# Layer norms of layers 2 and 3 computed inside the loops of the stages before them, on one Trainium2 core

## The chip, the cores and the metric

The kernel runs on one core of one Trainium2 chip. The metric is the device time of one execution in microseconds (us). TensorE multiplies matrices out of SBUF into PSUM, VectorE and ScalarE work elementwise and read PSUM, GpSimd works elementwise on SBUF, SyncE issues the DMAs. In the profile they are PE (PEld for its weight loads), DVE, ACT, POOL and SP.

## The reference

Eight residual steps on x (8 batches x 256 tokens x 128 channels) with a context of 8 x 512 x 96:

```
for l in 0..3:
    x = x + Ll_xattn(_layernorm(x), ctx, ...)
    x = x + Ll_ffn(_layernorm(x), ...)
_layernorm: (x - mean) / sqrt(var + 1e-5), over the 128 channels
```

Each step needs `_layernorm` of the x that the step before has left, token by token. Those that matter here:

- L1_ffn: 8 experts; each has a fixed block of 128 tokens in each of 2 halves of the token list. `h = gelu(g @ w1 + b1)`, `y = h @ w2 + b2`, `out = gelu(y @ next_w + next_b)`.
- L2_xattn: 8 heads of 64, `softmax(q k^T / 8) v`, then `@ Wo + bo`. L3_xattn is the same with 16 heads.
- L2_ffn: q and k projections, their images under W_inv, a running sum of k over the tokens, a router (gelu, then softmax over 8), and per expert `(q V) * (cumsum(k) W) * weight`, summed through U and projected by W_O.
- L3_ffn: the two best experts of 8 per batch, chosen by its first token's normed x; the mean of their two feed-forwards is added.

## The kernel before

All tokens stay in SBUF as `g.x`, 16 tiles of 128 tokens (partitions) x 128 channels. Every stage is one or more blocks. A block has a program for each engine, the engines keep in step by semaphores, and all of them meet at a block's end; behind each stage `clear_semaphores` (L110) runs a block of its own. Within an engine all instructions run in the order of the text.

Four stages begin with the norm of all 16 tiles by the class `AllTiles` (L214): VectorE computes statistics (`bn_stats`, L252, `bn_aggr`, L257) of two halves of 8 tiles and adds epsilon (L261), GpSimd raises to the power -1/2 (L289), VectorE subtracts the mean and scales (L268), TensorE transposes 4 tiles into one PSUM bank (L296). What comes then differs:

- `split_heads` (L1226), ahead of `wide_attention` in layers 2 and 3: ScalarE copies each bank to `z_hi` in the reduced type fp32r (L1256), VectorE subtracts for `z_lo` (L1264), and GpSimd splits the weights wq, wk and wv in two in the same way (3 casts, L1246, then 3 subtractions, L1249). These raw weights are loaded at the start of the run with all others.
- `l2_ffn` (L1824), block l2f_front: ScalarE copies 512 transposed tokens at a time to a small `zT` (L1972). TensorE's steps are skewed by chunk: transposes, then the q and k products (L1922), then the W_inv and router products, then the logits (L1928). VectorE makes the running sums (L2014). GpSimd zeroes the stacked weights (L1894) and splits four tables (L1899, L1902). The softmax of all tokens starts with L2040.
- `l3_ffn` (L2209), block l3f_norm: ScalarE copies the transposed tokens to `zT` and the first token of each batch to `zT_first` (L2255, L2256). Then the router's scores (L2242).

The loops ahead of them:

- `l1_ffn` (L1612). Its block l1f_front norms twice and makes xaT; there SyncE loads w1 and w2 of the first two experts (L1632). The block l1f_experts has 4 turns of 2 experts. TensorE's turn is second(u, 0) (L1742), next_layer(u - 1) (L1750, L1751), second(u, 1), then hidden(u + 1) for both experts (L1733); next_layer of the last turn follows the loop. ScalarE: the gelu of next_layer's result (L1780), then 8 gelus of hidden (L1775). VectorE: keep_y(u, 0) (L1799, writes yT), update(u - 1) of x (L1806, 4 tiles), keep_y(u, 1). GpSimd has nothing.
- `wide_attention` (L1268). 8 turns, one per batch (2 tiles), each of C = HEADS/2 units c (pairs of heads). A unit's work, 4 blocks of 128 x 512 scores, is a chain: scores (TensorE, L1377), maxima (VectorE, L1532), exponentials (ScalarE, L1479), reciprocals (VectorE, L1538), scaling (GpSimd, L1333), and in the next unit the transposes (`turned`, TensorE, L1386) and their copies (u = 0, 2 by VectorE, L1544; u = 1, 3 by ScalarE, L1486), one later the weighted sum (L1397) and its copy (L1549). Between these stand the projections of the next unit: k (L1353), q (L1345) and v (L1362), whose results are split by ScalarE (L1467, L1462) and VectorE (`k_low` L1527, `q_low` L1522). The output projection of batch b - 1 (`joined`, L1406) ends unit 1 of batch b on TensorE, the update of x (L1555) ends it on VectorE.
- `l2_ffn`, block l2f_experts: 4 turns of 512 tokens (4 tiles), each of 8 steps n. TensorE: the products of step n + 1 (L2096, L2100, L2103), then out(u, n) (L2110), which needs VectorE's `prod` of step n; output(u - 1) (L2121) after n = 1. ScalarE copies xv (L2148). VectorE multiplies twice a step (L2178, L2182), splits q and cum at n = 1 and n = 5 (L2172, L2173), and updates x at n = 3 (L2187). xv and prod have two buffers each. GpSimd has nothing.

The print below is of the kernel before; the profile's line numbers are its own.

## Time and profile before

| | us |
|---|---|
| time, median of 3 runs | 1837.53 (1837.08 to 1838.91) |
| the profiled execution's own time | 1838.08 |
| its span, first to last instruction | 1836.2 |
| TensorE busy (matmuls) | 1523.5, 83% of the span |
| TensorE weight loads | 1073.8, 58% |
| VectorE busy | 1043.0, 57% |
| ScalarE busy | 952.4, 52% |
| GpSimd busy | 596.4, 32% |
| mean granted TensorE clock | 0.899 of full |

A row of the timeline gives the start in us from the span's start, the duration, engine, line, operation, what it writes and reads with shapes, the number of instructions merged in it (xN), and in brackets the idle time of the engine before it and what ended it. The duration of a merged row runs from the first start to the last end. Ends of matmuls are modelled. A matmul of fp32 counts as two instructions. Tile names start with the stage: l1f, l2w (split_heads of layer 2), l2a, l2f, l3w, l3a, l3f.

### The profile page before, as it was taken

The page shows a single profiled execution, that of the slowest core. Times are in us where ns is not written, and L with a number is a line of the kernel's source. Part 1 is how long each engine was busy: PE and PEld are TensorE (multiplying, and loading weights), DVE is VectorE, ACT ScalarE, POOL GpSimd, SP SyncE. Part 2 cuts the span into 40 slices and gives each one's busy share as a digit, 9 for nine tenths or more (in the row PEclk, how much of TensorE's full clock was granted, in tenths as well). Part 3 has the DMA queues.
Part 4 walks back from the last instruction along what each step waited for, and adds up shares of the span by engine and source line. Part 5 has one row for each costly group of instructions (what it writes and reads, how often), then busy time and mean ns, then how long its engine had stood idle before and what let it go on. Part 6 is the DMA issues. An engine that isn't in the chain of part 4 may idle for free. (4 is left out here: it accounts for less than half of the span.)

```text
span 1836.2 us, 31074 instructions
## 1 busy us (share of the span) xinstructions
PE 1523.5 (83%) x10011; PEld 1073.8 (58%) x10011; DVE 1043.0 (57%) x2401; ACT 952.4 (52%) x2022; POOL 596.4 (32%) x592
## 2 busy tenths in 40 slices
PE   3999984698348736689999978959999999999976
PEld 2555543597125524567677746736777777777754
DVE  3566635344657654455665655665566666666651
ACT  2787861342356463265665623315666566665642
POOL 3323313100000001255555530034554554555441
PEclk7999995799569957789999988978999999999997
DMA  5300000000000002100000000000000000000002
GB/s 150 80 0 0 1 1 1 1 1 5 18 1 1 0 1 64 29 1 0 0 0 0 1 1 1 1 0 1 1 1 0 0 0 0 0 0 0 1 2 69
DMA packets 28737, 19.84 MB, mean 11 GB/s; under 512 B 9128, under 2 KB 25716, under 8 KB 28660
## 3 DMA queue, kind: packets, MB, share of 16 engines
q1 hardware_dynamic: 28660, 18.87, 3.7%
q8 instruction: 42, 0.69, 0.2%
q14 instruction: 35, 0.29, 0.0%
HBM read 17.81 MB, written 1.05 MB: 10 GB/s over the span
## 5 line engine op out<-in xcount | busy, mean ns | idle before, releaser
L1333 POOL TENSOR_TENSOR l3a_prob<-l3a_prob,l3a_rinv 128x512 f32<-128x512 f32 x256 | 260.8, 1040 | 249.9 <-DVE l3a_rinv L1538 245.0
L1479 ACT ACTIVATE l3a_prob<-l3a_scores_ps,l3a_nmax 128x512 f32<-128x512 f32 x256 | 173.2, 683 | 137.9 <-DVE l3a_nmax L1532 137.9
L1532 DVE TENSOR_REDUCE l3a_nmax<-l3a_scores_ps 128x2 f32<-128x1024 f32 x128 | 150.8, 1219 | 87.6 <-PE l3a_scores_ps L1377 87.5
L1333 POOL TENSOR_TENSOR l2a_prob<-l2a_prob,l2a_rinv 128x512 f32<-128x512 f32 x128 | 130.3, 1040 | 123.7 <-DVE l2a_rinv L1538 122.7
L746 ACT ACTIVATE l0a_prob<-l0a_scores_ps,l0a_k_scale 128x1024 f32<-128x1024 f32 x128 | 142.4, 1114 | 38.0 <-PE l0a_pv_ps L640 35.3
L1386 PE MATMUL l3a_turned_ps<-const,l3a_prob 128*128 128x128 f32 x1024 | 156.3, 276 | 3.0 <-DVE l3a_probT L1544 0.9
L1386 PEld LDWEIGHTS l3a_turned_ps<-const,l3a_prob 128*128 128x128 f32 x1024 | 118.4, 141 | 26.8 <-DVE l3a_probT L1544 11.9
L1397 PE MATMUL l3a_work_ps<-l3a_probT,l3a_v 128*64 128x256 f32 x1024 | 124.6, 385 | 1.6 <-ACT l3a_probT L1486 0.9
L1479 ACT ACTIVATE l2a_prob<-l2a_scores_ps,l2a_nmax 128x512 f32<-128x512 f32 x128 | 86.6, 683 | 73.7 <-DVE l2a_nmax L1532 73.7
L1544 DVE COPY l3a_probT<-l3a_turned_ps 128x512 f32<-128x512 f32 x128 | 87.8, 686 | 56.5 <-PE l3a_turned_ps L1386 56.4
L1532 DVE TENSOR_REDUCE l2a_nmax<-l2a_scores_ps 128x2 f32<-128x1024 f32 x64 | 75.5, 1219 | 41.2 <-PE l2a_scores_ps L1377 41.1
L1397 PEld LDWEIGHTS l3a_work_ps<-l3a_probT,l3a_v 128*64 128x64 f32 x1024 | 68.3, 136 | 51.9 <-issue 23.6
L626 PE MATMUL l0a_scores_ps<-l0a_qS,l0a_kS 128*128 128x512 f32 x256 | 91.7, 440 | 0.2
L289 POOL TENSOR_TENSOR l1f_front_all_rstd<-l1f_front_all_var_eps,neg_half 128x8 f32<-128x8 f32 x4 | 6.8, 1700 | 236.8 <-DVE l1f_front_all_var_eps L261 236.8
L640 PE MATMUL l0a_pv_ps<-l0a_prob,l0a_v 128*32 128x256 f32 x1024 | 81.7, 391 | 0.8 <-ACT l0a_prob L746 0.8
L1386 PE MATMUL l2a_turned_ps<-const,l2a_prob 128*128 128x128 f32 x512 | 78.0, 276 | 2.3 <-DVE l2a_probT L1544 0.9
L1486 ACT ACTIVATE l3a_probT<-l3a_turned_ps 128x512 f32<-128x512 f32 x128 | 76.9, 601 | 4.8 <-PE l3a_turned_ps L1386 4.8
L1172 ACT ACTIVATE l0f_experts_hidden<-l0f_experts_hidden_ps,vectors 128x512 f32<-128x512 f32 x64 | 43.0, 687 | 59.7 <-PE l0f_experts_hidden_ps L1133 59.5
L1386 PEld LDWEIGHTS l2a_turned_ps<-const,l2a_prob 128*128 128x128 f32 x512 | 58.8, 140 | 14.8 <-DVE l2a_probT L1544 6.5
L1196 DVE SCALAR_TENSOR_TENSOR l0f_experts_acc<-l0f_experts_y_ps,l0f_experts_gate_chunk,l0f_experts_acc 128x128 f32<-128x128 f32 x112 | 31.5, 344 | 59.7 <-PE l0f_experts_y_ps L1149 59.7
L1397 PE MATMUL l2a_work_ps<-l2a_probT,l2a_v 128*64 128x256 f32 x512 | 62.3, 385 | 1.6 <-ACT l2a_probT L1486 0.9
L1471 ACT ACTIVATE l3a_v<-l3a_work_ps 128x512 f32<-128x512 f32 x64 | 38.2, 597 | 48.9 <-PE l3a_work_ps L1364 48.9
(607 smaller groups left out, 3807.4 us busy)
## 6 DMA issues: line engine op xcount, KB each, us to landing
l1f_w<-in_L_ffn_w SPq DMA_DIRECT2D x16, 256.0 KB, 2.9
l3f_experts_w<-in_L_ffn_W SPq DMA_DIRECT2D x32, 64.0 KB, 1.9
ctx_rows<-in_ctx SPq DMA_DIRECT2D x1, 1536.0 KB, 7.2
w_l_w<-in_L_ffn_W SPq DMA_DIRECT2D x1, 1024.0 KB
out_x<-x_tokens SPq DMA_DIRECT2D x1, 1024.0 KB, 4.5
w_l_wq<-in_L_xattn_Wq SPq DMA_DIRECT2D x1, 512.0 KB
w_l_wo<-in_L_xattn_Wo SPq DMA_DIRECT2D x1, 512.0 KB
l1a_raw_f<-in_L_xattn_W_f SPq DMA_DIRECT2D x1, 512.0 KB, 4.3
```

The costliest lines, as they stand in the source:

```text
L626: last = e.matmul(sc[n % 2][:, half * 512:half * 512 + 512], kS[:, grp, t * P:(t + 1) * P], qS[:, grp, 2 * half:2 * half + 2, :], start=Tr ...
L640: last = e.matmul(pvps[grp % 2][32 * j:32 * j + 32, 0:T], v[:, t, GH * grp + j, :], prob[n % 2][:, j * T:(j + 1) * T], start=t == 0, stop= ...
L746: e.activation(prob[n % 2][:, :], sc[n % 2][:, :], ACT.Exp, scale=kscale[:, n % KT:n % KT + 1]).then_inc(m.prob_ready, 1)
L1172: e.activation(h[x % 4][:, f, :], hps[n % (2 * FT)][:, :], ACT.Gelu, bias=g.l0_b1[:, n:n + 1]).then_inc(m.act_ready, 1)
L1333: e.tensor_tensor(prob[n][:, :], prob[n][:, :], bcast(rinv[:, n:n + 1], [P, S]), ALU.mult).then_inc(m.prob_ready, 1)
L1386: last = e.transpose(tps[u % 2][:, t * P:(t + 1) * P], prob[slot(c, u)][:, t * P:(t + 1) * P], g.ident)
L1397: last = e.matmul(work[0][HD * h:HD * h + HD, 0:T], v[:, t, head], pT[c % 2][:, t, h, :], start=t == 0, stop=t == KT - 1, tile_position=(0 ...
L1471: e.activation(v[:, c % 2 * 2:c % 2 * 2 + 2, c // 2 * 256:(c // 2 + 1) * 256], work[1][:, :].rearrange("p (t d) -> p t d", t=2), ACT.Copy) ...
L1479: e.activation(prob[at][:, :], bank(u), ACT.Exp, bias=nmax[:, at:at + 1], accum_out=rsum[:, at:at + 1]).then_inc(m.exp_ready, 1)
L1486: e.activation(pT[c % 2][:, :, u % 2, u // 2 * P:u // 2 * P + P], tps[u % 2][:, :].rearrange("p (t q) -> p t q", q=P), ACT.Copy).then_inc( ...
L1532: e.tensor_reduce(nmax[:, at:at + 2], sps[:, i * 1024:(i + 1) * 1024].rearrange("p (h k) -> p h k", h=2), AX.X, ALU.max, negate=True).then ...
L1544: e.tensor_copy(pT[c % 2][:, :, u % 2, u // 2 * P:u // 2 * P + P], tps[u % 2][:, :].rearrange("p (t q) -> p t q", q=P)).then_inc(m.pT_kept ...
```

## The change

The class `Ahead` norms one turn's tiles inside the loop of the stage before, into tiles that outlive the stage: `g.z_hi` and `g.z_lo` where an attention follows, `g.zT` (float32) where a feed-forward follows. `split_heads` and the four uses of `AllTiles` in layer 2, layer 3 attention and layer 3 feed-forward are deleted. The wq, wk and wv of layers 2 and 3 are no longer in the first load: `SplitWeights` loads them in block l1f_front (six DMAs, after the four expert loads) and splits them on GpSimd in block l1f_experts (six casts, six subtractions). In the loops' order:

- l1_ffn: TensorE's transposes of turn u - 1 stand at the end of turn u, ScalarE's copy too, VectorE's statistics, scaling and low part behind keep_y(u, 1); the last group behind the loop. GpSimd's power of group 0 stands behind the splits.
- wide_attention: VectorE's statistics of batch b - 1 stand behind the update at the end of unit 1, the scaling in unit 2 before the reciprocals, GpSimd's power at the head of unit 2, TensorE's two transposes at the end of unit 2 into `turned0`'s bank, ScalarE's copy at the end of unit 2; the first transposes of unit 3 wait for that copy.
- l2_ffn: statistics after n = 4, scaling after n = 5, transposes and ScalarE's copy after n = 6, low part after n = 7, in the bank of output's result. Its block l2f_front has no norm, no zT copies and no z banks; `w_stacked` is now two tiles, in z_hi and z_lo. xv and xy lie in `g.zT`.
- l3_ffn: block l3f_norm starts with the scores, read from `g.zT` with a stride.

The core of the diff:

```diff
+class Ahead:
+    def __init__(self, s, g, tiles):
+        self.g, self.tiles = g, tiles
+        self.stats = s.sb("ahead_stats", [P, tiles, 6])
+        self.mv = s.sb("ahead_mean_var", [P, tiles, 2])
+        self.var = s.sb("ahead_var_eps", [P, tiles])
+        self.rstd = s.sb("ahead_rstd", [P, tiles])
+        self.held = s.sb("ahead_held", [P, 1])
+        self.z = s.sb("ahead_z", [P, tiles, D])
+        self.x_counted = s.sem("ahead_x_counted")
+        self.var_ready = s.sem("ahead_var_ready")
+        self.rstd_ready = s.sem("ahead_rstd_ready")
+        self.z_ready = s.sem("ahead_z_ready")
+        self.z_turned = s.sem("ahead_z_turned")
+        self.z_kept = s.sem("ahead_z_kept")
+        self.z_lo_ready = s.sem("ahead_z_lo_ready")
+    def statistics(self, e, n, x, updated, count):
+        e.wait_ge(updated, count)
+        e.memset(self.held[:, :], 0.0)
+        for i in range(self.tiles):
+            e.bn_stats(self.stats[:, i, :], x[i]).then_inc(self.x_counted, 1)
+        e.wait_ge(self.x_counted, 2 * self.tiles * n + self.tiles)
+        e.memset(self.held[:, :], 0.0)
+        for i in range(self.tiles):
+            e.bn_aggr(self.mv[:, i, :], self.stats[:, i, :]).then_inc(self.x_counted, 1)
+        e.wait_ge(self.x_counted, 2 * self.tiles * n + 2 * self.tiles)
+        e.tensor_scalar(self.var[:, :], self.mv[:, :, 1], EPS, None, ALU.add).then_inc(self.var_ready, 1)
+    def gpsimd(self, e, n):
+        e.wait_ge(self.var_ready, n + 1)
+        e.tensor_tensor(self.rstd[:, :], self.var[:, :], self.g.neg_half[:, 0:self.tiles], ALU.pow).then_inc(self.rstd_ready, 1)
+    def apply(self, e, n, x):
+        e.wait_ge(self.rstd_ready, n + 1)
+        for i in range(self.tiles):
+            e.tensor_scalar(self.z[:, i, :], x[i], self.mv[:, i, 0:1], self.rstd[:, i:i + 1], ALU.subtract,
+                            ALU.mult).then_inc(self.z_ready, 1)
+    def tensor(self, e, n, out):
+        e.wait_ge(self.z_ready, self.tiles * (n + 1))
+        for i in range(self.tiles):
+            last = e.transpose(out[:, i * P:(i + 1) * P], self.z[:, i, :], self.g.ident)
+        last.then_inc(self.z_turned, 1)
+    def keep(self, e, n, out, src):
+        e.wait_ge(self.z_turned, n + 1)
+        e.activation(out, src, ACT.Copy).then_inc(self.z_kept, 1)
+    def low(self, e, n, out, src, high):
+        e.wait_ge(self.z_kept, n + 1)
+        e.tensor_tensor(out, src, high, ALU.subtract).then_inc(self.z_lo_ready, 1)
...
+    def sync(self, sp):
+        for n in self.NAMES:
+            sp.dma_start(self.raw[n][:, :], self.a[f"L{n[0]}_xattn_W{n[1]}"]).then_inc(self.loaded, 16)
+    def gpsimd(self, e):
+        e.wait_ge(self.loaded, 16 * len(self.NAMES))
+        for n in self.NAMES:
+            hi, lo = self.g.split[n]
+            e.tensor_copy(hi[:, :], self.raw[n][:, :]).then_inc(self.w_hi_ready, 1)
+        for i, n in enumerate(self.NAMES):
+            hi, lo = self.g.split[n]
+            e.wait_ge(self.w_hi_ready, i + 1)
+            e.tensor_tensor(lo[:, :], self.raw[n][:, :], hi[:, :], ALU.subtract).then_inc(self.w_lo_ready, 1)
...
@@ -1326,6 +1374,8 @@
 
             def turn(b, more):
                 for c in range(C):
+                    if c == 2 and not is_first(b):
+                        ahead.gpsimd(e, b - 1)
                     for u in range(UNITS):
                         if u % 2 == 0:
                             e.wait_ge(m.rinv_ready, 2 * (C * b + c) + u // 2 + 1)
...
                 n = C * b + c
                 e.wait_ge(m.prob_ready, UNITS * n + u + 1)
                 wait(e, m.pT_kept_act if u % 2 else m.pT_kept_dve, 2 * n + u // 2)
+                if u == 0 and c == 2:
+                    wait(e, ahead.z_kept, b)
                 for t in range(KT):
                     last = e.transpose(tps[u % 2][:, t * P:(t + 1) * P], prob[slot(c, u)][:, t * P:(t + 1) * P], g.ident)
                 last.then_inc(m.turned, 1)
...
                         turned(*turn_c, 3)
+                    if c == 2 and not first:
+                        e.wait_ge(m.pT_kept_dve, 2 * n)
+                        ahead.tensor(e, b - 1, tps[0])
...
                     if c >= 2 or not first:
                         keep_o(b + (c - 2) // C, (c - 2) % C)
+                    if c == 2 and not first:
+                        ahead.apply(e, b - 1, tiles_of(b - 1))
                     invert(b, c, 0)
                     if turns_here:
                         keep_turned(*turn_c, 0)
...
                     if c == 1 and not first:
                         update(b - 1)
+                        ahead_statistics(b - 1)
...
                 for j in range(PAIR):
                     load(sp, 0, j, True)
                     load(sp, 0, j, False)
+                weights.sync(sp)
...
+            @block.gpsimd
+            def _(e):
+                weights.gpsimd(e)
+                ahead.gpsimd(e, 0)
+                with e.Fori(1, TURNS) as u:
+                    ahead.gpsimd(e, u)
+                e.wait_ge(weights.w_lo_ready, len(weights.NAMES))
+
...
                     if after:
                         hidden(u + 1, 0)
                         hidden(u + 1, 1)
+                    if before:
+                        turn_ahead(u - 1)
...
+                def ahead_statistics(u):
+                    ahead.statistics(e, u, tiles_of(u), m.x_updated, PAIR * (u + 1))
+                    ahead.apply(e, u, tiles_of(u))
...
                     keep_y(u, 0)
                     if before:
                         update(u - 1)
                     keep_y(u, 1)
+                    if before:
+                        ahead_statistics(u - 1)
+                        keep_z_low(u - 1)
 
                 turns(e, turn)
                 update(TURNS - 1)
+                ahead_statistics(TURNS - 1)
+                keep_z_low(TURNS - 1)
 
...
-                for step in range(TURNS + 3):
-                    if step < TURNS:
-                        if step >= 2:
-                            e.wait_ge(m.zT_ready, step - 1)
-                        front.tensor(e, step, zps[step % 2])
+                for step in range(1, TURNS + 3):
                     c = step - 1
                     if 0 <= c < TURNS:
-                        e.wait_ge(m.zT_ready, c + 1)
-                        product(g.l2_wqT, zT[c % 2][:, :], (m.q_kept, c + 1), m.q_ready)
-                        product(g.l2_wkT, zT[c % 2][:, :], (m.cum_kept, 2 * c + 2), m.k_ready)
+                        chunk = g.zT[:, c * W:(c + 1) * W]
+                        product(g.l2_wqT, chunk, (m.q_kept, c + 1), m.q_ready)
...
-            xv = [s.sb(f"xv{i}", [P, W]) for i in range(2)]
-            xy = [s.sb(f"xy{i}", [P, W]) for i in range(2)]
+            xv = [g.zT[:, i * W:(i + 1) * W] for i in range(2)]
+            xy = [g.zT[:, (2 + i) * W:(3 + i) * W] for i in range(2)]
...
                         out(u, n)
                         if n == 1 and before:
                             output(u - 1)
+                        if n == 6 and before:
+                            ahead.tensor(e, u - 1, ups)
...
                         if n == 3 and before:
                             update(u - 1)
+                        if n == 4 and before:
+                            ahead_statistics(u - 1)
+                        if n == 5 and before:
+                            ahead.apply(e, u - 1, tiles_of(u - 1))
+                        if n == 7 and before:
+                            keep_z_low(u - 1)
                         if n == 5 and after:
                             split(u + 1, 0)
 
```

## Rows read from the trace of the kernel before

**Rows 1.** The page: granted TensorE clock in tenths, 40 equal slices of the span.

```profile
PEclk7999995799569957789999988978999999999997
```

**Rows 2.** Busy time by stretch: length, PE, PEld, DVE, ACT, POOL busy, clock, DMA share, GB/s.

```profile
840.00:880.00 40.00, 39.15 (x286) 28.96 (x284) 24.36 (x46) 25.02 (x63) 23.80 (x24) 1.00 0.00 0
```

**Rows 3.** Waits, 1300 to 1760 us, layer 3 attention: total, times, longest us.

```profile
PEld l3a_work_ps L1362 <- DVE l3a_k_lo L1527: 8.5, 48, 0.2
```

**Rows 4.** Timeline: layer 1's experts and the start of layer 2's attention.

```profile
717.73 3.69 PE L1733 MATMUL l1f_experts_h_ps<-l1f_xaT,l1f_w 128*128 128x256 f32 x16 [1.20 <-PEq L1635]
...
747.19 0.48 DVE L1799 TENSOR_SCALAR l1f_experts_yT<-l1f_experts_y_ps,vectors 128x256 f32<-128x256 f32 x1 [0.51 <-PE l1f_experts_y_ps L1742]
...
750.32 1.89 PE L1742 MATMUL l1f_experts_y_ps<-l1f_experts_h,l1f_w 128*128 128x256 f32 x8
...
757.30 0.48 DVE L1799 TENSOR_SCALAR l1f_experts_yT<-l1f_experts_y_ps,vectors 128x256 f32<-128x256 f32 x1 [0.53 <-PE l1f_experts_y_ps L1742]
757.84 0.49 PE L1750 MATMUL l1f_experts_o_ps<-w_l_next_w,l1f_experts_yT 128*128 128x128 f32 x2 [0.58 <-DVE l1f_experts_yT L1799]
...
761.94 0.76 DVE L1806 TENSOR_TENSOR x_tokens<-x_tokens,l1f_experts_og 128x256 f32<-128x256 f32 x2 [4.15 <-ACT l1f_experts_og L1780]
...
779.85 0.55 PE L1345 MATMUL l2a_work_ps<-l2h_z_hi,l2h_wq_hi 128*128 128x256 f32 x1 [1.88 <-PEq L1230]
```

**Rows 5.** Timeline: end of layer 2's attention, front of its feed-forward.

```profile
1068.35 0.29 DVE L1555 TENSOR_TENSOR x_tokens<-l2a_work_ps,x_tokens 128x128 f32<-128x128 f32 x1 [1.21 <-PE l2a_work_ps L1407]
...
1078.77 1.91 PE L1922 MATMUL l2f_front_ring_ps<-l2f_front_zT,w_l_wqT 128*128 128x512 f32 x2
...
1086.60 2.41 DVE L2014 TENSOR_TENSOR_SCAN l2f_cum<-l2f_front_ones,l2f_front_ring_ps 128x256 f32<-128x256 f32 x4
...
1111.21 0.42 DVE L2040 TENSOR_TENSOR l2f_front_biased<-l2f_front_logits_ps,l2f_front_bias 128x256 f32<-128x256 f32 x1 [0.52 <-PE l2f_front_logits_ps L1928]
```

**Rows 6.** Timeline: layer 2's experts and the start of layer 3's attention.

```profile
1157.92 0.69 DVE L2182 TENSOR_TENSOR l2f_experts_prod<-l2f_experts_xy,l2f_experts_weights_ps 128x512 f32<-128x512 f32 x1
...
1163.79 0.60 ACT L2148 ACTIVATE l2f_experts_xv<-l2f_experts_xv_ps 128x512 f32<-128x512 f32 x1 [1.87 <-PE l2f_experts_xv_ps L2096]
...
1164.50 1.02 PE L2110 MATMUL l2f_experts_out_ps<-l2f_experts_prod,l_uT 128*128 128x512 f32 x2
...
1213.15 0.69 DVE L2187 TENSOR_TENSOR x_tokens<-l2f_experts_update_ps,x_tokens 128x512 f32<-128x512 f32 x1 [3.98 <-PE l2f_experts_update_ps L2121]
...
1235.78 0.55 PE L1345 MATMUL l3a_work_ps<-l3h_z_hi,l3h_wq_hi 128*128 128x256 f32 x1 [1.89 <-PEq L1230]
```

**Rows 7.** Timeline: end of layer 3's attention, first scores of its feed-forward.

```profile
1782.63 0.29 DVE L1555 TENSOR_TENSOR x_tokens<-l3a_work_ps,x_tokens 128x128 f32<-128x128 f32 x1 [2.10 <-PE l3a_work_ps L1407]
...
1794.91 0.21 PE L2242 MATMUL l3f_norm_scores_ps<-w_l_wr,l3f_zT_first 128*8 128x8 f32 x2 [0.75 <-ACT l3f_zT L2256]
```

**Rows 8.** Timeline: two-tile norm, layer 0 attention; groups by line: a four-column power.

```profile
226.75 0.49 DVE L861 BATCH_NORM_STATS2 l0a_y_stats<-l0a_y 128x6 f32<-128x128 f32 x2
...
228.53 0.60 DVE L872 TENSOR_SCALAR l0a_y<-l0a_y,l0a_y_mean_var,l0a_y_rstd 128x128 f32<-128x128 f32 x2 [0.81 <-POOL l0a_y_rstd L482]
...
L473 POOL TENSOR_TENSOR l0a_k_scale_next<-l0a_k_clamped,neg_half 128x4 f32<-128x4 f32 x8 | 8.8, 1101 | 6.1 <-DVE l0a_k_clamped L805 6.0
```

**Rows 9.** Timeline: statistics and scalings ahead of layer 3's two stages.

```profile
1219.44 13.28 DVE L268 TENSOR_SCALAR l3w_all_z<-x_tokens,l3w_all_mean_var,l3w_all_rstd 128x128 f32<-128x128 f32 x16
...
1784.21 1.64 DVE L252 BATCH_NORM_STATS2 l3f_norm_all_stats<-x_tokens 128x6 f32<-128x128 f32 x8 [1.28 <-PEq L120]
...
1788.80 4.19 DVE L268 TENSOR_SCALAR l3f_norm_all_z<-x_tokens,l3f_norm_all_mean_var,l3f_norm_all_rstd 128x128 f32<-128x128 f32 x16
```

**Rows 10.** Timeline: unit 2 of the second batch in layer 3's attention.

```profile
1326.76 2.36 DVE L1532 TENSOR_REDUCE l3a_nmax<-l3a_scores_ps 128x2 f32<-128x1024 f32 x2 [0.51 <-PE l3a_scores_ps L1377]
...
1330.02 0.60 PE L1386 MATMUL l3a_turned_ps<-const,l3a_prob 128*128 128x128 f32 x4
...
1330.65 0.69 DVE L1544 COPY l3a_probT<-l3a_turned_ps 128x512 f32<-128x512 f32 x1 [0.83 <-PE l3a_turned_ps L1386]
```

More of the change, by code:

```diff
@@ L1339, in _ @@
             turns(e, turn)
+            ahead.gpsimd(e, B - 1)
         @block.tensor
@@ L1567, in turn @@
                         keep_o(b + (c - 2) // C, (c - 2) % C)
+                    if c == 2 and not first:
+                        ahead.apply(e, b - 1, tiles_of(b - 1))
                     invert(b, c, 0)
@@ L1845, in l2_ffn @@
             s = Scope(nc, ctx, "l2f_front")
-            front = AllTiles(s, g)
-            zT = [s.sb(f"zT{i}", [P, W]) for i in range(2)]
             hT = [[s.sb(f"hT{r}{i}", [P, W]) for i in range(2)] for r in range(2)]
@@ L2162, in turn, with keep_z @@
                             split(u + 1, 0)
+                        if n == 6 and before:
+                            keep_z(u - 1)
+                def keep_z(u):
+                    ahead.keep(e, u, tokens_of(g.z_hi, u), ups[:, :])
                 split(0, 0)
@@ L3267, in build @@
                 for_l0.close()
-            if stage is l2_ffn:
-                for_l2.close()
         store_stage(nc, g, a)
```

221 lines of the change are left out of this document (114 added, 107 removed).

## The prediction

> **What bounds the kernel now.** I read the page first: the row of TensorE's granted clock dips in slices 17 and 18, 24 and 25, 27 and 28, and the last [rows 1]. Then busy time by stretch: inside layer 2's attention TensorE works 39.15 of 40 us at full clock [rows 2], and the wait table of the later attention shows it held only in short waits on VectorE, 8.5 us in 48 of them for the low part of the keys [rows 3]. So the loops are bound by TensorE, with VectorE close behind. Then the timelines of the four stage borders, where the dips are. There TensorE waits for the norm of all tokens. The next stage's first projection starts 779.85 - 762.70 = 17.2 us after layer 1's last token update (761.94 + 0.76) [rows 4], 1078.77 - 1068.64 = 10.1 us after layer 2 attention's [rows 5], 1235.78 - 1213.84 = 21.9 us after layer 2 feed-forward's [rows 6], and 1794.91 - 1782.92 = 12.0 us after layer 3 attention's [rows 7]. Sum 61 us: the ceiling of what the change can touch. The profiled execution took 1838.08 us around a span of 1836.2; the median is 0.55 us lower. I work against 1838.08.
>
> **What stays at each border.** The last group of tokens still needs its norm after its update. Layer 0's attention has the same sequence for two tiles: statistics start at 226.75, the scaled tokens at 228.53, so 1.78 us, and 0.60 for the two scalings [rows 8]. Four tiles add two statistics (8 take 1.64, so 0.41 [rows 9]), at most 0.25 for their aggregation, and a longer power on GpSimd (1.10 and 0.1 of hand-over, where VectorE idled 0.81 here, so 0.40 [rows 8]); 0.1 for the added memsets is an estimate. So 2.9 us to the scaling, and four scalings at 4.19/16 = 0.26 [rows 9] make 4.0. Four transposes take 0.60 at full clock [rows 10], 1.2 at half; ScalarE's copy 0.60 [rows 6]; VectorE's low part 0.69 [rows 6], needed before an attention only. A border with semaphore clears takes 1784.21 - 1782.92 = 1.3 us [rows 7, 9].
>
> Layer 2 feed-forward to layer 3 attention: 4.0 + 1.2 + 0.6 + 0.7 + 0.2 of hand-overs + 1.3 = 8.0 us instead of 21.9. **Gain 14.0.** Much of the old 21.9 is no norm at all: the 16 scalings lasted 13.28 us there against 4.19 at layer 3's feed-forward, because GpSimd split the weights beside them [rows 9]. The Trainium skill (SBUF — State Buffer, Who interferes with whom) says that the two engines share a port pair as an exclusive lock, which the loser waits for; these two rows agree with it.
>
> Layer 3 attention to feed-forward, two tiles: 1.9 + 0.6 (scalings) + 0.6 (transposes at half clock) + 0.4 (half-width copy, estimate) + 1.3 = 4.8 instead of 12.0. **Gain 7.2.**
>
> Layer 2 attention to feed-forward: the first product starts after 4.8 instead of 10.1 us, gain 5.3. The first scan stood behind VectorE's slow scalings until 1086.60 [rows 5]; now the first query and key products, 1.91 each at half clock [rows 5], follow 1068.64 + 4.8 = 1073.4, and the scan could start at 1077.2, 9.4 us earlier. TensorE then becomes the bound: of the work before 1111.21 it had done four products (0.95 each at full clock, half of 1.91) ahead of that scan, which now lie behind it, less two groups of transposes (0.6 each) that are gone. 9.4 - 3.8 + 1.2 = 6.8; two extra small VectorE instructions (the stacked weights are now two tiles) cost 0.3. I take 6.5, between 5.3 and 9.4. The zeroing and table splits on GpSimd start earlier too and are wanted only after the softmax. **Gain 6.5.**
>
> Layer 1 feed-forward to layer 2 attention: nothing, see next. The six raw weights (1.9 MB by their shapes, behind the first four expert loads on SP's queue) load beside layer 1's front and leave the first load. Their splits stand on GpSimd ahead of the first power. Layer 3's six took about the 13.28 us of that stretch [rows 9], layer 2's are half as wide: 20 us at most, from the loop's start at 717.73, and the first power is due a turn before 747.19 [rows 4], at about 738. I cost them at nothing; if the raw weights came 5 us into the loop, the first turn would wait for them.
>
> **What the loops pay.**
> (a) Layer 1's experts, 4 turns. The transposes stand last in TensorE's turn, behind the scalings, which follow the yT copy. In turn 2 that copy ends at 747.19 + 0.48 = 747.67, scaled tokens come 4.0 later, transposes end at 752.3, and second(3, 0) ran at 750.32 [rows 4]: 2.0 late. Turn 1 the same. In turn 3 nothing covers it: copy done at 757.78, scaled at 761.8, transposes until 762.7, and only then next_layer(3), which started at 757.84 [rows 4]: 4.9 late. Then the last group: its update ends 762.70 + 4.9 = 767.6, plus 4.0 + 1.2 + 0.6 + 0.7 + 0.2 = 774.3, plus the 4.0 of the turns = 778.3, plus 1.3 = 779.6, where 779.85 was. **Gain 0**, between +4 (turns hidden) and -4 (next_layer's 3.4 us at half clock).
>
> (b) Layer 2's and layer 3's attention, in 7 of 8 turns each: two transposes, 0.3 at full clock, certain since TensorE is full. VectorE gets the statistics (0.9 for two tiles, 1.2 with memsets and addresses) before the maxima of unit 2, where it had 0.51 idle [rows 10]: the maxima are 0.7 late. Then 0.6 of scaling before the reciprocal; 0.83 were idle ahead of its copy of the turned probabilities [rows 10], so 0.4 to 0.5 are left over, and they meet the low part of the keys, for which TensorE already waits [rows 3]. Later in the unit VectorE has idle time and catches up. The new wait of TensorE for that copy is already fulfilled when the fourth transposes are out; behind ScalarE's copy stand the exponentials, which wait for maxima anyway. 0.3 + 0.5 + 0.05 = 0.85 a turn, x14. **Loss 12**, between 0.3 x 14 = 4 and (1.2 + 0.6 + 0.3) x 14 = 29.
>
> (c) Layer 2's experts, 3 turns. After the product of step 4 (ends 1158.61 [rows 6]) the statistics of four tiles, 1.7, end at 1160.3; step 5's two multiplies (2 x 0.69 and a hand-over) end 1161.75, in time. Then 1.05 of scaling, 1.3 of splits (two more of that size), step 6's multiplies: 1165.6, and TensorE wanted that product at 1164.50 [rows 6]: 1.1 lost. The transposes cost 0.6. ScalarE's copy of z waits for them with the copy of step 7's xv queued behind it: that ran at 1163.79 [rows 6], now at 1167.4; step 7's product is ready at 1169.5, 0.85 after TensorE could use it. 2.55 in two turns; in the last, without splits, 2.1. **Loss 7.2**, between 1.8 (transposes alone) and 12 (all of VectorE's 1.7 + 1.05 + 0.7 and the transposes).
>
> Sum: 14.0 + 7.2 + 6.5 + 0 - 12 - 7.2 = 8.5 gained: 1838.08 - 8.5 = **1829.5 us**.
>
> **Rivals.** Within 0.2% (3.7 us) a measurement of this kernel can't tell a change from none.
> B, the loops absorb it: only the transposes cost in the attentions (4 instead of 12) and a little in the experts (4 instead of 7). 1829.5 - 8 - 3 = 1818. For it: VectorE is busy in 24.36 of 40 us [rows 2]. Against: the waits [rows 3] are at the very place that gets the delay.
> C, VectorE becomes the bound of the attention: the statistics before the maxima and the scalings before the reciprocal reach the end of each changed unit whole, 2.1 us instead of 0.85: 14 x 1.25 = 17.5 more, 1847. It decides from about 1.5 us a turn (9 more). For it: maxima, exponentials, GpSimd's scaling and transposes are one chain. Against: the idle 0.51 and 0.83 [rows 10].
> D, the clock: TensorE now stands 4 us before next_layer(3) and about 1 us at places in the experts of layer 2, and the granted clock was low in stretches behind idle TensorE [rows 1]. next_layer and transposes at half clock, 3.4 + 0.6, and some 2.5 in layer 2's experts: 1836, no difference.
> E, the port: in the attentions the scalings fall beside GpSimd's work on the probabilities. One costs 0.83 instead of 0.26 [rows 9]: 28 x 0.57 = 16, 1845. In these loops GpSimd is idle there, since its next work waits for the reciprocal behind the scalings. The rule of the Trainium skill named above would make it so wherever the two meet in time.
>
> **How the numbers follow.** Forecast 0.57 (its own range 1823 to 1834), B 0.14, D 0.15, C 0.10, E 0.04. Faster by over 0.2%: 0.57 + 0.14 = 0.71; within: 0.15; slower: 0.14. The range from 1818 (B) to 1841 holds D and half the way to C; what is left out is most of C and E and the edge of B. That the change does not do what it says is no rival: the four norm blocks are deleted from the text.
>
> **What would show it.** Right: from last update to first projection about 8, 5 and 8 us, and 17 in layer 1's if its turns are counted in; a pair of transposes and a VectorE lateness of 0.4 to 0.5 us in unit 2 of each attention turn, units 3 on unchanged; xv of step 7 some 3.5 us late in layer 2's experts; layer 1's expert loop 9 us longer. The forecast falls if a changed attention turn is longer by under 0.4 or over 1.5 us, if next_layer(3) starts without waiting, or if GpSimd's splits still run when the first power is due.

## The result, and the profile after the change

| | before | after |
|---|---|---|
| median of the runs | 1837.3 us (4 runs) | 1822.3 us (4 runs, 1818.3 to 1822.7) |
| ratio after / before | | 0.9912, 95% interval 0.9895 to 0.9929 |
| profiled execution: time, span | 1838.08, 1836.2 us | 1822.32, 1820.5 us |
| one turn (batch) of layer 2's attention | 34.38 us | 34.84 us |
| one turn of layer 3's attention | 66.54 us | 66.80 us |

The medians differ by 15.0 us (0.82%); the ratio is that of the means, which differ by 16.1. The forecast was 1829.5 us, a gain of 8.0 us on the 1837.53 that was known. The sign was right and the size was little over half: 1822.3 lies inside the range from 1818 to 1841 and 0.7 us below the 1823 to 1834 that the prediction gave the forecast itself, between it and rival B's 1818.

The page of the changed kernel, granted clock in 40 slices of its span, beside [rows 1]:

```profile
PEclk7999995799559957889999998988999999999997
```

Slices 17, 24 and 27, where layer 1's feed-forward, layer 2's attention and layer 2's feed-forward end, are each a tenth higher and slice 12 is a tenth lower; the dips are still there.

The timeline of the changed kernel in layer 1's experts and at the start of layer 2's attention, which answers to [rows 4] (L350, L355 and L359 are the lines of `Ahead`):

```profile
714.84 3.69 PE L1815 MATMUL l1f_experts_h_ps<-l1f_xaT,l1f_w 128*128 128x256 f32 x16 [1.20 <-PEq L1697]
...
750.90 1.89 PE L1824 MATMUL l1f_experts_y_ps<-l1f_experts_h,l1f_w 128*128 128x256 f32 x8
...
757.88 0.48 DVE L1893 TENSOR_SCALAR l1f_experts_yT<-l1f_experts_y_ps,vectors 128x256 f32<-128x256 f32 x1 [0.54 <-PE l1f_experts_y_ps L1824]
...
762.99 0.63 PE L1832 MATMUL l1f_experts_o_ps<-w_l_next_w,l1f_experts_yT 128*128 128x128 f32 x2
...
768.72 0.60 ACT L1868 ACTIVATE l1f_experts_og<-l1f_experts_o_ps 128x512 f32<-128x512 f32 x1 [4.89 <-PE l1f_experts_o_ps L1833]
769.35 0.76 DVE L1900 TENSOR_TENSOR x_tokens<-x_tokens,l1f_experts_og 128x256 f32<-128x256 f32 x2 [4.80 <-ACT l1f_experts_og L1868]
...
777.30 0.55 PE L1396 MATMUL l2a_work_ps<-z_hi,l_wq_hi 128*128 128x256 f32 x1 [2.26 <-PEq L120]
```

The yT copy ends at 758.36, and next_layer(3) starts only at 762.99: the transposes of group 2 stand before it. From there to ScalarE's copy at 768.72 it takes 5.7 us at a granted clock of 0.50, where it took 3.5 before the change, at 0.98.

The timeline around the end of layer 2's attention, beside [rows 5]; the first row is the second tile's update:

```profile
1069.61 0.29 DVE L1621 TENSOR_TENSOR x_tokens<-l2a_work_ps,x_tokens 128x128 f32<-128x128 f32 x1 [1.21 <-PE l2a_work_ps L1460]
...
1074.46 2.05 PE L2025 MATMUL l2f_front_ring_ps<-zT_of_l_attention,w_l_wqT 128*128 128x512 f32 x2 [1.38 <-PEq L120]
...
1078.25 1.26 DVE L2107 TENSOR_TENSOR_SCAN l2f_cum<-l2f_front_ones,l2f_front_ring_ps 128x256 f32<-128x256 f32 x2 [1.39 <-PE l2f_front_ring_ps L2025]
...
1104.24 0.42 DVE L2133 TENSOR_TENSOR l2f_front_biased<-l2f_front_logits_ps,l2f_front_bias 128x256 f32<-128x256 f32 x1 [0.52 <-PE l2f_front_logits_ps L2031]
```

A middle turn and the end of layer 2's experts, with the start of layer 3's attention, beside [rows 6]:

```profile
1159.65 1.12 PE L2219 MATMUL l2f_experts_out_ps<-l2f_experts_prod,l_uT 128*128 128x512 f32 x2 [0.49 <-DVE l2f_experts_prod L2301]
...
1160.61 0.60 PE L350 MATMUL l2f_experts_update_ps<-const,l2f_experts_ahead_z 128*128 128x128 f32 x4
...
1161.34 0.60 ACT L355 ACTIVATE z_hi<-l2f_experts_update_ps 128x512 f32 x1 [4.92 <-PE l2f_experts_update_ps L350]
1161.83 1.08 ACT L2261 ACTIVATE zT_of_l_attention<-l2f_experts_xv_ps 128x512 f32<-128x512 f32 x2
...
1163.98 0.70 PE L2219 MATMUL l2f_experts_out_ps<-l2f_experts_prod,l_uT 128*128 128x512 f32 x1 [1.14 <-DVE l2f_experts_prod L2301]
...
1211.55 1.22 PE L2219 MATMUL l2f_experts_out_ps<-l2f_experts_prod,l_uT 128*128 128x512 f32 x1 [2.67 <-DVE l2f_experts_prod L2301]
...
1217.06 0.69 DVE L2306 TENSOR_TENSOR x_tokens<-l2f_experts_update_ps,x_tokens 128x512 f32<-128x512 f32 x1 [4.97 <-PE l2f_experts_update_ps L2230]
...
1225.41 0.55 PE L1396 MATMUL l3a_work_ps<-z_hi,l_wq_hi 128*128 128x256 f32 x1 [2.72 <-PEq L120]
```

Both waits of TensorE that the forecast named are there: 0.49 us for step 6's product and 1.14 for step 7's, the second because ScalarE's copy of xv stands behind its copy of z. In the last turn the wait is 2.67 us, and the matmul behind it takes 1.22 where the one at 1163.98 took 0.70: the granted clock is 0.50 from 1211.5 to 1214.7.

The end of layer 3's attention, beside [rows 7]:

```profile
1773.90 0.29 DVE L1621 TENSOR_TENSOR x_tokens<-l3a_work_ps,x_tokens 128x128 f32<-128x128 f32 x1 [2.10 <-PE l3a_work_ps L1460]
...
1778.47 0.20 PE L2365 MATMUL l3f_norm_scores_ps<-w_l_wr,zT_of_l_attention 128*8 128x8 f32 x2 [1.36 <-PEq L120]
```

These rows cut the execution into stretches (all from the start of one row to the start of the next one named):

| stretch | before | after | gain | forecast |
|---|---|---|---|---|
| start to layer 1's first expert product | 717.73 | 714.84 | 2.9 | 0 |
| from there to layer 2 attention's first projection | 62.12 | 62.46 | -0.3 | 0 |
| layer 2's attention, to its last update | 288.50 | 292.31 | -3.8 | -6 |
| to the softmax of layer 2's router | 42.86 | 34.63 | 8.2 | 6.5 |
| to the last update of layer 2's experts | 101.94 | 112.82 | -10.9 | -7.2 |
| to layer 3 attention's first projection | 22.63 | 8.35 | 14.3 | 14.0 |
| layer 3's attention, to its last update | 546.85 | 548.49 | -1.6 | -6 |
| to layer 3's router scores | 12.28 | 4.57 | 7.7 | 7.2 |
| to the end of the span | 41.29 | 42.03 | -0.7 | 0 |
| sum | | | 15.8 | 8.5 |

The borders came out as forecast. The miss of 7.3 us is 6.6 in the attentions, 2.9 at the start, 1.7 in the front and 0.8 at two borders, less 3.7 in layer 2's experts and 0.3 and 0.7 elsewhere.

Unit 2 of the second batch in layer 3's attention after the change, beside [rows 10]. The unit begins behind the last token update of the first batch, at 1315.51 here and at 1325.96 before:

```profile
1316.76 2.35 DVE L1595 TENSOR_REDUCE l3a_nmax<-l3a_scores_ps 128x2 f32<-128x1024 f32 x2
...
1319.36 0.59 DVE L344 TENSOR_SCALAR l3a_ahead_z<-x_tokens,l3a_ahead_mean_var,l3a_ahead_rstd 128x128 f32 x2
...
1320.20 0.69 DVE L1607 COPY l3a_probT<-l3a_turned_ps 128x512 f32<-128x512 f32 x1 [0.17 <-PE l3a_turned_ps L1439]
...
1320.81 0.68 DVE L1590 TENSOR_TENSOR l3a_k_lo<-l3a_work_ps,l3a_k_hi 128x512 fp32r<-128x512 f32 x1
...
1322.81 0.39 PE L350 MATMUL l3a_turned_ps<-const,l3a_ahead_z 128*128 128x128 f32 x2
```

The maxima start 1.25 us after the update, where it was 0.80: 0.45 late, not 0.7. The copy of the turned probabilities starts 4.69 us after it, exactly as before (1330.65 - 1325.96), and still has 0.17 us of idle time ahead. So nothing of VectorE's lateness reaches the keys: their low part starts 5.30 us after the update, as before (1331.26). What does come later, by 0.66 us, is the first reciprocal between the two (4.36 us after the update, before 3.71, 1319.87 and 1329.67), and GpSimd's scaling of the probabilities with it. The wait table over 1300 to 1760 us says the same as [rows 3], to the digit:

```profile
PEld l3a_work_ps L1413 <- DVE l3a_k_lo L1590: 8.5, 48, 0.2
```

### The profile page after: what moved, and what is told of

It reads as the page before. It is cut to its first block and busy times, and to the rows that moved or that the text cites. A ratio compares the mean times of both kernels' runs of the same rounds, so it can differ in the third digit from the quotient of the medians.

```text
span 1820.5 us, 31249 instructions
## 1 busy us (share of the span) xinstructions
PE 1520.2 (84%) x10011; PEld 1070.5 (59%) x10011; DVE 1030.3 (57%) x2467; ACT 950.6 (52%) x2026; POOL 601.8 (33%) x610
## 5 line engine op out<-in xcount | busy, mean ns | idle before, releaser
L1234 PEld LDWEIGHTS l0f_experts_y_ps<-w_l_w,l0f_experts_hidden 128*128 128x128 f32 x512 | 61.5, 192 | 2.7
```

Source lines behind the costliest of these rows:

```text
L1234: last = e.matmul(out, h[x % 4][:, f, tokens], g.l0_w2[:, x, f, :], start=f == 0, stop=f == FT - 1)
```

## The experiments

**1. The norm taken out of the two expert loops.** A stage `norm_stage` stands ahead of each attention (the norm of all 16 tiles and the two halves of z, as before the change, but no weights); the expert loops of layers 1 and 2 lose everything of `Ahead`.

```
 def l3_attention(nc, g, a):
+    norm_stage(nc, g, "l3n")
     wide_attention(nc, g, "l3a", 16, ...
...
-                        if n == 4 and before:
-                            ahead_statistics(u - 1)
-                        if n == 5 and before:
-                            ahead.apply(e, u - 1, tiles_of(u - 1))
-                        if n == 7 and before:
-                            keep_z_low(u - 1)
```

> The changed kernel with the norm taken out of the expert loops of layers 1 and 2 and put back as a stage of its own ahead of each attention; the weights stay split in layer 1's feed-forward, and the norms inside the attention loops stay. Theory (at these two borders it was the early split that paid; the norm inside the expert loops costs more than it saves): layer 2's expert loop falls from 100.7 us (first product to last update) to about 90, its turn from 24.2 to 21.6; the border behind it, first projection after the last update's start, is 21.9 less the 9.1 by which the scalings were slowed = 12.9 instead of 7.7; layer 1's last update is 10.3 earlier in its loop and its border about 12.5 instead of 7.2 us. Sum 5.5 + 5 gained: about 1812. Rival (the norm in the loops made the border short; without it 21.9 and 17.2 us come back, whoever splits the weights): about 1825.

Measured: 1813.1 us (4 runs, 1810.95 to 1815.0), 0.9863 of before (0.9845 to 0.9881), where about 1812 were expected. Timeline of this kernel at the two borders:

```profile
762.07 0.76 DVE L1918 TENSOR_TENSOR x_tokens<-x_tokens,l1f_experts_og 128x256 f32<-128x256 f32 x2 [4.15 <-ACT l1f_experts_og L1892]
...
768.60 4.19 DVE L268 TENSOR_SCALAR l2n_all_z<-x_tokens,l2n_all_mean_var,l2n_all_rstd 128x128 f32<-128x128 f32 x16
...
775.84 0.55 PE L1396 MATMUL l2a_work_ps<-z_hi,l_wq_hi 128*128 128x256 f32 x1 [1.88 <-PEq L1663]
...
1204.62 0.69 DVE L2295 TENSOR_TENSOR x_tokens<-l2f_experts_update_ps,x_tokens 128x512 f32<-128x512 f32 x1 [3.98 <-PE l2f_experts_update_ps L2229]
...
1217.97 0.35 PE L1396 MATMUL l3a_work_ps<-z_hi,l_wq_hi 128*128 128x256 f32 x1 [2.20 <-PEq L1663]
```

The theory holds. With no weights split beside them the sixteen scalings take 4.19 us, not 13.28 [rows 9]. The border to layer 3's attention is 13.35 us between starts: 9.3 of the 14.3 us gained there came from the weights, and 5.0 from the norm in the loop. That norm costs the loop more than 5.0: here it lasts from 1113.48 (first product) to 1204.62, 91.1 us, and with the norm 100.7. At layer 1's end the border is 13.77 us between starts, 1.3 more than expected, against 17.91 before and 7.95 with the norm in the loop; the last update comes 44.2 us after the loop's start instead of 54.5. There the split earned 4.1 us, and the norm in the loop cost 10.3 for 5.8. At these two borders the early split earned the gain, and the moved norm, in the order that the change gave it, lost part of it again.

**2. The norm stays in all loops, in another order.**

```
                     if after:
                         hidden(u + 1, 0)
                         hidden(u + 1, 1)
-                    if before:
+                    if before and after:
                         turn_ahead(u - 1)
...
                 next_layer(TURNS - 1)
+                turn_ahead(TURNS - 2)
                 turn_ahead(TURNS - 1)
...
-                        if n == 6 and before:
+                        if n == 7 and before:
                             keep_z(u - 1)
...
-                        if n == 3 and before:
+                        if n == 2 and before:
                             update(u - 1)
+                        if n == 3 and before:
+                            count(u - 1)
                         if n == 4 and before:
-                            ahead_statistics(u - 1)
+                            gather(u - 1)
```

`count` and `gather` are the two halves of `statistics`; the two subtractions of VectorE's split of the next group stand in steps 4 and 6 instead of both in step 5, and ScalarE's half of it in step 3. In layer 1 ScalarE keeps z of group 2 behind the last gelu, and VectorE's low part of it fills the wait for the last power.

> The changed kernel with the norm still in all loops but placed otherwise in two of them. Layer 1's experts: the transposes of the last but one group stand behind the last next_layer on TensorE. Layer 2's experts: ScalarE keeps step 7's xv before z; VectorE's update, statistics, variance, scaling and the halves of the split are spread over steps 2 to 6. Theory (the losses in these loops are order, not work): the last next_layer starts 4.6 us earlier and at full clock, 3.4 instead of 5.7 us, so 6.9 gained; the turn of layer 2's experts falls from 24.2 to 22.3 us (transposes and a hand-over left of 2.6), the last one by 3.4: 7 gained. About 1808.5. Rival (VectorE's added work itself bounds layer 2's turn): the turn stays at 24 us and only 6.9 are gained, 1815.5. Rival (TensorE is idle around the last next_layer anyway, so it stays at half clock): 2.3 less in either case.

Measured: 1804.69 us (5 runs, 1804.22 to 1805.42), 0.982 of before (0.9807 to 0.9834). Its timeline:

```profile
715.93 3.69 PE L1815 MATMUL l1f_experts_h_ps<-l1f_xaT,l1f_w 128*128 128x256 f32 x16 [1.20 <-PEq L1697]
...
757.76 0.49 PE L1832 MATMUL l1f_experts_o_ps<-w_l_next_w,l1f_experts_yT 128*128 128x128 f32 x2 [0.58 <-DVE l1f_experts_yT L1895]
...
769.79 0.55 PE L1396 MATMUL l2a_work_ps<-z_hi,l_wq_hi 128*128 128x256 f32 x1 [2.26 <-PEq L120]
...
1161.96 0.68 DVE L2317 TENSOR_TENSOR x_tokens<-l2f_experts_update_ps,x_tokens 128x512 f32 x1
...
1183.99 0.68 DVE L2317 TENSOR_TENSOR x_tokens<-l2f_experts_update_ps,x_tokens 128x512 f32<-128x512 f32 x1
...
1200.59 0.69 DVE L2317 TENSOR_TENSOR x_tokens<-l2f_experts_update_ps,x_tokens 128x512 f32<-128x512 f32 x1 [2.75 <-PE l2f_experts_update_ps L2235]
```

next_layer(3) starts as soon as the yT copy lets it, at a granted clock of 1.00 (757.7 to 761.2) instead of 0.50, so the rival of the half clock falls. Layer 1's experts to the first projection: 53.9 us instead of 62.5; executions with the changed kernel's order there took 60.4 to 62.5, so 6.5 to 8.6 us are gained. The turn of layer 2's experts is 22.03 us where it was 24.2, and 21.58 before the change: all that is left of the norm is 0.45 us a turn, less than the 0.60 of its transposes. So the loss was the order, not the work, and the rival (VectorE's work as the bound) falls too. The gain, 17.6 us on the changed kernel, is 3.8 more than expected. Some of it is how executions differ: the first turn of layer 2's experts, in which the clock is low for a while, varies by 1.5 us with the same code (see below).

**3 and 4. VectorE's added work done twice in the attentions.** Two statistics more ahead of the maxima, or two scalings more ahead of the reciprocal; results that nobody reads.

```
             def ahead_statistics(b):
                 ahead.statistics(e, b, tiles_of(b), m.x_updated, TPB * (b + 1))
+                for i in range(TPB):
+                    e.bn_stats(again_stats[:, i, :], tiles_of(b)[i])
```

```
                         ahead.apply(e, b - 1, tiles_of(b - 1))
+                        for i in range(TPB):
+                            e.tensor_scalar(again_z[:, i, :], ...
```

> The changed kernel with the two statistics of each attention turn executed twice (a second result tile, read by nobody): 0.5 us more of VectorE ahead of the maxima of unit 2. The prediction's step (VectorE's lateness reaches the low part of the keys and with it TensorE): the turn grows by 0.5, from 34.83 to 35.3 in layer 2 and from 66.80 to 67.3 in layer 3, 14 x 0.5 = 7 us in all. Rival (VectorE's idle time between the maxima and the low part takes it up): turns unchanged within 0.1, time unchanged.

> The changed kernel with the two scalings of each attention turn executed twice (a second tile, read by nobody): 0.5 us more of VectorE between the maxima and the first reciprocal of unit 2. The prediction's step: the turn grows by 0.5, in layer 2 from 34.83 to 35.3 and in layer 3 from 66.80 to 67.3, 7 us in all. Rival (idle time takes it up): VectorE had 0.17 us idle left ahead of its copy of the turned probabilities, so the low part of the keys is 0.3 to 0.35 us later; if TensorE's wait for it is bound by ScalarE's high part instead, the turns are unchanged within 0.1.

**5. The two transposes of each attention turn done twice.**

```
                         e.wait_ge(m.pT_kept_dve, 2 * n)
+                        e.wait_ge(ahead.z_ready, TPB * b)
+                        for i in range(TPB):
+                            e.transpose(tps[0][:, i * P:(i + 1) * P], ahead.z[:, i, :], g.ident)
                         ahead.tensor(e, b - 1, tps[0])
```

> The changed kernel with the two transposes of each attention turn executed twice. Theory (TensorE is full there, so what it is given costs whole; this is nearly all that a turn pays): 0.26 to 0.3 us more a turn, 66.80 to 67.1 in layer 3 and 34.83 to 35.1 in layer 2. Rival (the 0.26 of layer 3 is VectorE's lateness and the transposes fill a gap of TensorE): turns unchanged within 0.05.

One run each: 1824.11, 1826.33 and 1822.38 us. The turns decide more sharply than the times. A turn is a quarter of the time between the first batch's last update and the fifth's; these are the rows of the changed kernel, then of the fourth experiment:

```profile
835.16 0.29 DVE L1621 TENSOR_TENSOR x_tokens<-l2a_work_ps,x_tokens 128x128 f32 x1 [1.21 <-PE l2a_work_ps L1460]
...
974.51 0.29 DVE L1621 TENSOR_TENSOR x_tokens<-l2a_work_ps,x_tokens 128x128 f32 x1 [1.21 <-PE l2a_work_ps L1460]
...
1315.51 0.29 DVE L1621 TENSOR_TENSOR x_tokens<-l3a_work_ps,x_tokens 128x128 f32 x1 [2.10 <-PE l3a_work_ps L1460]
...
1582.70 0.29 DVE L1621 TENSOR_TENSOR x_tokens<-l3a_work_ps,x_tokens 128x128 f32 x1 [2.10 <-PE l3a_work_ps L1460]
```

```profile
835.13 0.29 DVE L1623 TENSOR_TENSOR x_tokens<-l2a_work_ps,x_tokens 128x128 f32 x1 [1.21 <-PE l2a_work_ps L1460]
...
976.57 0.29 DVE L1623 TENSOR_TENSOR x_tokens<-l2a_work_ps,x_tokens 128x128 f32 x1 [1.21 <-PE l2a_work_ps L1460]
...
1318.06 0.29 DVE L1623 TENSOR_TENSOR x_tokens<-l3a_work_ps,x_tokens 128x128 f32 x1 [2.10 <-PE l3a_work_ps L1460]
...
1586.18 0.29 DVE L1623 TENSOR_TENSOR x_tokens<-l3a_work_ps,x_tokens 128x128 f32 x1 [2.10 <-PE l3a_work_ps L1460]
```

| us | turn, layer 2 | turn, layer 3 | layer 2: from a batch's last update to GpSimd's low half of the next context |
|---|---|---|---|
| before | 34.38 | 66.54 | 10.00 |
| changed | 34.84 | 66.80 | 10.47 |
| statistics twice | 35.20 | 67.10 | 10.80 |
| scalings twice | 35.36 | 67.03 | 10.98 |
| transposes twice | 34.83 | 67.01 | 10.46 |
| context copy early (experiment 6) | 34.14 | 66.32 | 9.71 |

Neither side of experiments 3 and 4 holds as it was put. Half a us more of VectorE costs 0.23 to 0.52 us a turn, so the idle time is nearly used up; what the change itself added went into it. In both experiments the keys' low part now starts later (5.56 and 5.54 us after the update instead of 5.30): the way that the prediction gave the delay is there, and the change's own delay was too short for it. In layer 3 the transposes' second copy costs 0.21, about the 0.26 that the turn had grown: there the price is nearly all the transposes. In layer 2 they cost nothing, and my expectation of 0.3 was wrong. The waits of TensorE's matmuls say why. Total, times and longest wait, over four turns of layer 2 (830 to 970 us), of the kernel before, the changed one, and the fourth experiment:

```profile
PE l2a_work_ps L1353 <- POOL l2a_c_lo L1325: 1.6, 4, 0.4
```

```profile
PE l2a_work_ps L1404 <- POOL l2a_c_lo L1373: 2.5, 4, 0.6
```

```profile
PE l2a_work_ps L1404 <- POOL l2a_c_lo L1373: 3.7, 4, 0.9
```

And where one such instruction of GpSimd starts, behind the update at 905.51 before the change and at 904.83 after it:

```profile
915.51 1.26 POOL L1325 TENSOR_TENSOR l2a_c_lo<-l2a_cT,l2a_c_hi 96x512 fp32r<-96x512 f32 x1
```

```profile
915.30 1.27 POOL L1373 TENSOR_TENSOR l2a_c_lo<-l2a_cT,l2a_c_hi 96x512 fp32r<-96x512 f32 x1
```

In layer 2 (4 units a batch) GpSimd splits the next context right behind its scaling of unit 2's probabilities, the unit that the norm delays. The reciprocal comes later, GpSimd's scaling with it, and TensorE waits for the context's low half 0.2 us longer each turn after the change, and 0.5 longer with the scalings done twice; with the transposes done twice it waits 0.4 again, as before the change. The last column of the table says the same more sharply: in all six kernels layer 2's turn is 24.4 us longer than the way from the update to that instruction, whatever was added and where. In layer 3 (8 units) the split stands behind unit 6, and that wait is 0.4 us in all of them. In the third experiment the wait that grows is the one that I had forecast for the change itself: for the keys' low part, in the same stretch, 3.7 us in 16 weight loads where the changed kernel has 3.0 in 17. In the fourth, in layer 3 (1300 to 1760 us), it is the transposes' wait for VectorE's copy of the turned probabilities, 1.5 us in 7 instead of 0.4 in 1.

**6. GpSimd's copy of the next context ahead of the scaling.** It tests that reading in the changed kernel.

```
             def turn(b, more):
                 for c in range(C):
                     if c == 2 and not is_first(b):
                         ahead.gpsimd(e, b - 1)
+                    if c == C - 2 and more:
+                        take_ctx(b + 1)
```

`take_ctx` is the copy (0.61 us) with its wait, cut off from the top of `split_ctx`.

> The changed kernel with one instruction of GpSimd moved in both attentions: the copy of the next batch's context (0.61 us) stands ahead of unit C-2's scaling of the probabilities, where GpSimd is idle, instead of behind it. Theory (layer 2's turn grew by 0.45 and layer 3's by 0.26 because in layer 2 the split of the context stands right behind the scaling of the unit that the norm delays, and TensorE waits for its low half, 0.6 us a turn in layer 2 and 0.4 in layer 3): both waits go, and the turns fall to about 34.25 and 66.4. Rival (that wait is covered by another that ends just behind it, such as the copy of unit 3's keys): turns fall by under 0.1.

Measured: 1810.45 us in one run; the turns are 34.14 and 66.32 us, 0.70 and 0.48 less than in the changed kernel. The wait has left TensorE's matmuls in both layers. The reading holds, with somewhat more gained than expected. Layer 2's turn is shorter than before the change, so the move also takes away a wait that the kernel before had; it is no measure of the norm's part alone.

**7. The changed kernel once more, unchanged.**

> The changed kernel as it is, once more. Theory (the 2.9 us by which layer 1's experts started earlier than before the change are no effect of it: the same code started them at 717.86 in one kernel above and at 714.84 in another): the start falls somewhere between 714.8 and 717.9, and from there to the end the execution takes as long as the first one, 1105.7 of its 1820.5 us, within 2. Rival (the shorter load brings it): 714.8 again within 0.5.

Measured: 1820.07 us. Layer 1's experts start here:

```profile
715.99 3.69 PE L1815 MATMUL l1f_experts_h_ps<-l1f_xaT,l1f_w 128*128 128x256 f32 x16 [1.20 <-PEq L1697]
```

The first execution had 714.84, experiment 1 had 717.86 with the same code up to there, and before the change it was 717.73 [rows 4]. The shorter first load starts nothing sooner: TensorE's first matmul of layer 0's attention stands at 30.31 us before the change and at 30.53 in the changed kernel. So the rival falls, and the 2.9 us at the start are how executions differ. The rest took 1102.3 us, 3.4 less than in the first execution and more than the 2 allowed: 2.1 of it in layer 1's experts, 1.3 in layer 2's attention. Any single stretch of the table above carries 1 to 3 us of this kind, above all where the clock falls; the turns inside the attentions repeat within 0.03 us in the four executions with that code.

**8. Experiments 2 and 6 together.**

> The order of the second experiment and GpSimd's copy of the context moved as in the sixth. If both theories hold, 7 x 0.6 and 7 x 0.4 come on top: 1804.7 - 7 = 1797.7. If the context's wait is covered by another one: 1804 to 1805.

Measured: 1798.92 us (5 runs, 1794.63 to 1800.15), 0.9785 of before (0.9771 to 0.9798), 1.2 from what was expected if both hold: the fastest version, 39 us ahead of the kernel before in the same runs (1837.99) and 23 ahead of the changed one. Its turns are 34.15 and 66.35 us.

## Why the forecast was right in sign and short in size

**The borders held.** Between last update and next stage 8.35, 4.85 and 4.57 us were measured from the update's start, 7.7, 4.6 and 4.3 from its end; forecast were 8.0, 4.8 and 4.8. The sum of small terms (statistics, power, scalings, transposes, copies, clears) taken from two-tile and sixteen-tile rows was good to 0.5 us each. That the slow scalings came from GpSimd's splits beside them was argued, and experiment 1 showed it: 4.19 us without the splits. The Trainium skill's rule on the shared port pair (SBUF — State Buffer, Who interferes with whom) has one of the two engines wait while the other holds the pair; these runs agree with it, with 13.28 against 4.19.

**The attentions are the step that failed.** Loss (b) had 0.85 us a turn; measured are 0.26 in layer 3 and 0.46 in layer 2, 7 x 0.72 = 5.0 in the turns instead of 12. The term that was wrong is "0.4 to 0.5 are left over, and they meet the low part of the keys". It was a small difference of larger numbers, each rounded to the dear side. Statistics with memsets: 1.2 taken, 0.96 measured (from the update's end at 1315.80 to the maxima). The idle time before the changed places: 0.51 and 0.83 counted, but the copy of o between them had 0.22 of its own, which I did not look up. 0.96 + 0.59 of work against 1.56 of idle time leaves nothing over. This was rival B's mechanism. What I held against it, "the waits are at the very place that gets the delay", is true only of a delay that reaches that place. By the prediction's own criterion the forecast fell here: layer 3's changed turn is longer by under 0.4 us.

**The transposes, "certain since TensorE is full", were certain in one layer only.** In layer 2 TensorE waited for GpSimd each turn, and the transposes went into that wait. The norm still cost 0.46 there, on another way: reciprocal, GpSimd's scaling, context, whose low half starts 10.47 instead of 10.00 us after the update. The 39.15 us of 40 [rows 2] hid a wait of 0.4 us in 34.

**Layer 2's experts: the mechanism was right, and the rest is the clock.** The middle turns grew by 2.63 us (24.2 less 21.58) where 2.55 were forecast. Both waits named are there, 0.49 and 1.14 where 1.1 and 0.85 were forecast, which leaves 1.0 for the transposes and hand-overs instead of 0.6: the close sum is in part luck. The last turn grew by 4.2 instead of 2.1, and the first, which has no norm in it, by 1.5. The kernels of experiments 3 to 7 have the same loop. In experiment 6 the last product was waited for as long (2.68 us), the granted clock stayed at 1.00 behind it, and the turn took 16.59 us, 2.65 more than before the change; in the five executions in which the clock fell it took 17.9 to 18.1. The first turn took 34.15 at a mean granted clock of 0.91 in the changed kernel, 32.64 at 0.96 before it, and 32.62 and 32.71 at 0.96 and 0.95 in experiments 3 and 6. So the order costs 7.9 us in the three turns where 7.2 were forecast, and 3 us of the 10.9 are falls of the clock that another execution of the same loop doesn't show. Rival D had 2.5 us for this, and gave them to the whole change as a case of its own instead of to the sum.

**Layer 1's experts: nothing gained, as forecast.** next_layer(3) waited 4.6 us, 4.9 were forecast, and it ran at half clock besides, 2.3 us that only the bound had in it. Against these stood 3.5 us instead of 4.0 in the turns before, and a border behind it of 7.2 us from the update's end where the sum gave 8.0. That they cancel to 0 is luck. The prediction's end of the transposes, 762.7, is 0.3 later than its own 761.8 + 0.6. GpSimd's splits, priced at nothing, ended at 730.1, 5.9 us before the first power.

**The front gained 8.2 us instead of 6.5.** The scan starts 9.6 us earlier after the update, as forecast within 0.2, but the way from scan to softmax grew by 1.4 us, not by the 2.9 of the products that now lie behind the scan. TensorE's busy time in it did grow by 2.8 (23.17 to 25.95 us). The missing term is a wait that the kernel before had there (1086.6 to 1111.2 us):

```profile
PE l2f_front_ring_ps L1922 <- DVE l2f_cum L2014: 1.6, 1, 1.6
```

With the scans no longer stacked behind VectorE's scalings it is gone: TensorE is idle for 1.4 us of this way before and for none of it after.

**The start: 2.9 us that no step of the change explains,** and that another execution of the same code does not show (experiments 1 and 7). Without them the profiled pair differs by 12.9 us.

Rival C (VectorE the bound of the attention) was wrong for this change, though experiments 3 and 4 show how near it was: the next half microsecond costs. Rival E fell by the row at 1319.36: two scalings in 0.59 us, as without a neighbour.

## What to carry to other kernels

Work moved into a full loop costs what it does at its place in each engine's order: the same norm cost layer 2's experts 2.6 us a middle turn in one order and 0.45 in another. Before pricing a delay, add up all the idle time between the place that is delayed and the place that waits, and follow every engine that the delayed one feeds, not only the one whose wait is largest. When a change does two things, ask of each gain which of the two it came from; here the early split of the weights paid at borders where the moved norm, as ordered, lost.

## What the runs showed that I had not expected

With identical code up to layer 1's experts, their start varied from 714.84 to 718.29 us over the nine profiled executions of changed versions, and part of it appears already at the end of layer 0's attention: its last update fell at 277.08 in the changed kernel and at 278.60 before it, where the windows from 265 to 275 us show the clock at 0.96 and 0.50 before, and at 1.00 and 0.77 after. The time at which the granted clock falls moves by some us from one execution to the next while the work does not. The Trainium skill (TensorE: Matmul & The Clock Gate, What's actually happening) says that the window by which the gate judges TensorE's activity runs freely and does not start with the kernel; the varying starts above agree with that and do not prove it.

An engine that looked full (TensorE at full clock, 98% busy by its windows) took two more transposes a turn in layer 2 without getting slower, the same two that cost 0.21 us a turn in layer 3, and gave 0.70 us a turn back when a single copy of 0.61 us on GpSimd was moved.
